# The later layers' pieces in the attention: two parts behind a first half's scores, or four lots behind a second half's

## What is computed

```python
x = inputs.reshape(B, T, NUM_HEADS, HEAD_DIM).transpose(0, 2, 1, 3)
q = x * rotation_params[None, :, None, :]
k = x * entangle_params[None, :, None, :]
attn_weights = jax.nn.softmax(jnp.einsum('bhid,bhjd->bhij', q, k) * scale, axis=-1)
out = jnp.einsum('bhij,bhjd->bhid', attn_weights, x)
...
x = x + _layernorm(_L0_attn_ref(_layernorm(x), ...))   # 4 batches x 16 heads
x = x + _layernorm(_L0_ffn_ref(_layernorm(x), ...))    # token mix, W_r, W_k, relu squared, W_v
x = x + _layernorm(_L1_attn_ref(_layernorm(x), ...))   # linear attention q, k, v, then a 1024-wide MLP
x = x + _layernorm(_L1_ffn_ref(_layernorm(x), ...))    # gate, up, down
```

## Time and profile before

| | us |
|---|---|
| median of 3 runs | 3210.76 (3210.0 to 3214.39) |
| span of the profiled execution | 3210.7 |
| attention, to the last exponential | about 2008 |
| busy: PE, ACT, DVE | 2925.7, 2332.2, 1481.2 |

### The profile page before, as it was taken

One profiled execution on the slowest core, in us unless ns is written; L12 is line 12 of the kernel. 1 busy time (PEld: TensorE's weight loads), 2 busy tenths in 40 slices (PEclk: granted clock), 3 DMA queues, 4 the chain that ended last, 5 costly groups with the idle time before them and its releaser, 6 DMA issues. The chain is left out here.

```text
span 3210.7 us, 48004 instructions
## 1 busy us (share of the span) xinstructions
PE 2925.7 (91%) x18048; PEld 1172.8 (37%) x18048; DVE 1481.2 (46%) x3536; ACT 2332.2 (73%) x2586; POOL 214.9 (7%) x193
## 2 busy tenths in 40 slices
PE   1998998999999999999999999489999999999986
PEld 0221221222222222222222222266666666666654
DVE  6221220322441333232421311668888888866574
ACT  2999999999999999999999999223343334333332
POOL 0000000000000000000000000111111111111110
PEclk9999999999999999999999999699999999999998
DMA  3411111311211221111210110221122111111010
GB/s 115 141 41 36 59 39 36 101 37 35 89 37 35 83 68 42 57 42 43 69 55 28 45 42 21 81 66 53 53 78 66 59 59 59 46 56 50 26 47 21
DMA packets 125601, 177.69 MB, mean 55 GB/s; under 512 B 42248, under 2 KB 100616, under 8 KB 125128
## 3 DMA queue, kind: packets, MB, share of 16 engines
q1 hardware_dynamic: 122392, 172.53, 16.7%
q10 hardware_dynamic: 2992, 2.23, 0.2%
HBM read 107.62 MB, written 67.11 MB: 54 GB/s over the span
## 5 line engine op out<-in xcount | busy, mean ns | idle before, releaser
L717 ACT ACTIVATE probs<-ps 128x1024 f32<-128x1024 f32 x2048 | 1894.4, 1173 | 87.0 <-PE ps L456 83.6
L585 PE MATMUL ps<-probs,vals 128*32 128x512 f32 x8192 | 1094.2, 607 | 0.0
L456 PE MATMUL ps<-qT,kT 64*128 64x512 f16 x4096 | 730.3, 387 | 109.8 <-DMA kT<-split_dram 28.1
L456 PEld LDWEIGHTS ps<-qT,kT 64*128 64x128 f16 x4096 | 173.5, 93 | 1152.0 <-ACT probs L717 1025.3
L872 DVE COPY sums<-ps 128x512 f32<-128x512 f32 x64 | 44.3, 692 | 502.3 <-PE ps L585 502.3
L585 PEld LDWEIGHTS ps<-probs,vals 128*32 128x32 f32 x8192 | 162.0, 108 | 294.2 <-issue 232.8
L1310 PE MATMUL layers_ps<-yT,weight_mem 128*128 128x512 f32 x512 | 227.6, 595 | 11.2 <-ACT hT L1551 10.0
L1316 PE MATMUL layers_ps<-weight_mem,hT 128*128 128x256 f32 x1024 | 231.5, 380 | 0.0
L1578 ACT ACTIVATE gate<-layers_ps 128x512 f32<-128x512 f32 x96 | 57.3, 597 | 224.9 <-PE layers_ps L1464 224.8
L1316 PEld LDWEIGHTS layers_ps<-weight_mem,hT 128*128 128x128 f32 x1024 | 193.0, 190 | 29.8
L1464 PE MATMUL layers_ps<-n4T,weight_mem 128*128 128x512 f16 x768 | 176.7, 384 | 7.3 <-DVE n4T L1801 7.3
(11 more groups left out here) (224 smaller groups left out, 2607.6 us busy)
## 6 DMA issues: line engine op xcount, KB each, us to landing
split_dram<-parts SPq DMA_DIRECT2D x28, 768.0 KB, 3.7
qT<-split_dram SPq DMA_DIRECT2D x126, 128.0 KB
kT<-split_dram SPq DMA_DIRECT2D x126, 128.0 KB
heads_dram<-result SPq DMA_DIRECT2D x64, 128.0 KB, 7.4
q_in<-q_dram SPq DMA_DIRECT2D x16, 512.0 KB, 3.3
n_in<-n_dram SPq DMA_DIRECT2D x16, 512.0 KB, 3.4
x_in<-x_dram SPq DMA_DIRECT2D x16, 512.0 KB, 5.2
out_dram<-y_out SPq DMA_DIRECT2D x16, 512.0 KB, 4.3
```

Of the source, the lines that this page charges most:

```text
L456: last = nc.tensor.matmul(SCORES[slot][:, n * BANK:(n + 1) * BANK], kT[buf][rows, j * P:(j + 1) * P], qT[buf][rows, q0:q0 + BANK], start=T ...
L585: mm = nc.tensor.matmul(ACC[32 * c:32 * c + 32, :], vals[buf][:, j, :], probs[:, j % PROBS, c * BANK:(c + 1) * BANK], start=(j == 0), stop ...
L717: nc.scalar.activation(probs[:, j % PROBS, half * T // 2:(half + 1) * T // 2], SCORES[slot_of(at)], ACT.Exp, scale=OPERAND_SCALE ** -2).th ...
```

## The change

`PART_GAP = 3` gives way to `LOTS_AT = (0, 1, 3, 4)`. A piece now goes to PE in four lots of half the size of a part, and each lot stands behind the second half's scores of a block: the starting block, the next, and the ones three and four later. A lot of a matmul piece is one matmul of 256 columns (two records), one of `kv` is two, one of a transposing piece is one transpose. The second and fourth lots complete what the first and third began in the bank.

```diff
-PART_GAP = 3
+LOTS_AT = (0, 1, 3, 4)
...
-                half = TURN.rearrange("p (b n) -> p b n", b=2)[:, part, :]
+                first, second = part // 2, part % 2
+                half = TURN.rearrange("p (b n) -> p b n", b=2)[:, first, :]
...
-                        for k in range(K4):
-                            last = nc.tensor.transpose(TURN[:, k * P:(k + 1) * P], src[:, k, h * P:(h + 1) * P], ident[:, :])
-                        last.then_inc(fr_full, 1)
-                    return
+                    last = nc.tensor.transpose(TURN[:, part * P:(part + 1) * P], src[:, part, h * P:(h + 1) * P], ident[:, :])
...
-                    for k in range(KC):
-                        last = tok_out(half, fr_uT, 2 * int(stage[-1]) + part, w, k)
+                    last = tok_out(half, fr_uT, 2 * int(stage[-1]) + first, w, second)
...
-                if part == 1:
+                if part == len(LOTS_AT) - 1:
                     last.then_inc(fr_full, 1)
...
-                    for part in range(2):
-                        step = front_step(head, j - PART_GAP * part)
-                        if half == 0 and step is not None:
-                            front(step, part, head, rounds_at(head, j - PART_GAP * part))
+                    for part, after in enumerate(LOTS_AT):
+                        step = front_step(head, j - after)
+                        if half == 1 and step is not None:
+                            front(step, part, head, rounds_at(head, j - after))
```

More of the change, by code:

```diff
@@ L521, in front @@
                         pe.wait_ge(ready, c + 1)
-                        for k in range(K4):
-                            last = nc.tensor.transpose(TURN[:, k * P:(k + 1) * P], src[:, k, h * P:(h + 1) * P], ident[:, :])
-                        last.then_inc(fr_full, 1)
-                    return
-                if stage in ("mix_r0", "mix_r1"):
+                    last = nc.tensor.transpose(TURN[:, part * P:(part + 1) * P], src[:, part, h * P:(h + 1) * P], ident[:, :])
+                elif stage in ("mix_r0", "mix_r1"):
                     if part == 0:
@@ L529, in front @@
                         pe.wait_ge(layer_sem("mixed"), c + 1)
-                    for k in range(KC):
-                        last = tok_out(half, fr_xr, 2 * int(stage[-1]) + part, W["wr"], k)
+                    last = tok_out(half, fr_xr, 2 * int(stage[-1]) + first, W["wr"], second)
                 elif stage in ("mix_k0", "mix_k1"):
                     i = int(stage[-1])
-                    last = nc.tensor.matmul(TURN, W["wk"][:, part, i * P:(i + 1) * P], fr_xk[:, part, :], start=(part == 0), stop=(part == KC - 1))
+                    last = nc.tensor.matmul(half, W["wk"][:, second, i * P:(i + 1) * P], fr_xk[:, second, first * N // 2:(first + 1) * N // 2],
+                                            start=(second == 0), stop=(second == KC - 1))
                 elif stage in ("val0", "val1"):
@@ L537, in front @@
                         pe.wait_ge(layer_sem("k_act_done"), c + 1)
-                    for k in range(KC):
-                        last = tok_out(half, fr_kact, 2 * int(stage[-1]) + part, W["wv"], k)
+                    last = tok_out(half, fr_kact, 2 * int(stage[-1]) + first, W["wv"], second)
                 elif stage in ("k0", "k1", "v0", "v1"):
@@ L543, in front @@
                     w = W["akv"][:, :, 0:C] if stage[0] == "k" else W["akv"][:, :, C:2 * C]
-                    for k in range(KC):
-                        last = tok_out(half, fr_uT, 2 * int(stage[-1]) + part, w, k)
+                    last = tok_out(half, fr_uT, 2 * int(stage[-1]) + first, w, second)
                 elif stage in ("q0", "q1"):
                     i = int(stage[-1])
-                    last = nc.tensor.matmul(TURN, W["aq"][:, part, i * P:(i + 1) * P], fr_uT[:, part, :], start=(part == 0), stop=(part == KC - 1))
+                    last = nc.tensor.matmul(half, W["aq"][:, second, i * P:(i + 1) * P], fr_uT[:, second, first * N // 2:(first + 1) * N // 2],
+                                            start=(second == 0), stop=(second == KC - 1))
                 elif stage == "kv":
@@ L552, in front @@
                         pe.wait_ge(layer_sem("k_feat_done"), c + 1)
-                    for k in range(K4):
-                        last = nc.tensor.matmul(TURN[:, part * KVW:(part + 1) * KVW], fr_k[:, k, part * P:(part + 1) * P], fr_v[:, k, part, :],
+                    for k in range(second * K4 // 2, (second + 1) * K4 // 2):
+                        last = nc.tensor.matmul(TURN[:, first * KVW:(first + 1) * KVW], fr_k[:, k, first * P:(first + 1) * P], fr_v[:, k, first, :],
                                                 start=(k == 0), stop=(k == K4 - 1))
-                if part == 1:
+                if part == len(LOTS_AT) - 1:
                     last.then_inc(fr_full, 1)
```

## The result

| | before | after |
|---|---|---|
| median of 4 runs, us | 3212.57 (3210.0 to 3216.24) | 3224.98 (3223.09 to 3229.99) |
| span of the profiled execution | 3210.7 | 3224.0 |
| heads 18 to 63 without 31 and 47 | 1330.46 | 1348.11 |
| heads 31 and 47 | 71.46 | 70.12 |
| behind the attention | 1202.7 | 1201.0 |

The changed kernel takes 1.0041 of the time before (95% interval 1.0027 to 1.0055), 12.4 us more. 3231 was forecast, with 3215 to 3240 around it. A head's time is the distance between the ends of the last exponentials of two heads; heads 31 and 47, which hold the branches to other code, stand apart.

The account below looks back on a forecast made before the run. ACT's own pace, 29.33 us a head, bounds the attention; about 32 us are waits for scores. Block 2 3.6, rounds 2.6, block 10 2.7 and the head's end 10.8 make 19.7, about +20 on 3210.7: 3231, range 3215 to 3240.

Parts of the forecast that it names:

- block 2: 33 pieces starting in block 2: lots lose 0.58 us a piece for 0.39 to 0.53, together +3.6.
- block 10 with the head's end: 19 pieces starting in block 10: +2.7 us for their own losses, +10.8 where the last lot meets the head's end.
- the 19.7: Sum of the forecast's terms in us: 3.6 + 2.6 + 2.7 + 10.8, taken as +20 on 3210.7.
- The lot's cost: Each matmul lot on PE delays the value product by 0.64 us, a transposing lot about 0.27; weight loads not hidden.
- the cheap lots: Rival: fixed cost of entering and leaving is hidden, a lot costs +0.43 us; 12 us faster, 3199; chance 0.08.
- the reserve: A first half's scores may start 0.78 us late before ACT loses time; PE makes up 0.30 a block.
- Rounds: In 9 heads with a round behind a block-2 piece, block 8's transposes lose 0.29 us each: +2.6.
- The late read: Head's end, 9 block-10 pieces with two-instruction reads: DVE copies the sums some 0.5 us late; 5 to 6 in all.
- A read too late: Rival: block-2 pieces finish later and DVE's chain moves, costing 1 to 2 us in 6 heads; 3240; chance 0.08.
- the operands' copies next: Under the late-read rival: head 35's room of 1.2 us holds narrowly, with these DVE copies next in line.
- ACT's own activations: Heads 37, 59, 61, 63: activations right behind their input's last lot may wait up to 0.5 us each, left to the range.

Follow-up runs that it names:

- gap4: Kernel before, with the second part of block-2 matmul pieces in heads without a round four blocks behind the first instead of three: 3208.14 us, 0.9989.
- block2_lots: Changed kernel's lots only for pieces that start in block 2; those starting in block 10 go in two parts as before: 3220.25 us, 1.0022 of before.
- lots_first_half: Changed kernel with its four lots behind the first half's scores instead of the second's: 3232.57 us, 1.0063 of before.
- block10_lots: Changed kernel's lots only for pieces that start in block 10; those starting in block 2 go in two parts as before: 3223.0 us, 1.0036 of before.
- lots_0123: Changed kernel with lots behind blocks 0, 1, 2 and 3 instead of 0, 1, 3 and 4: 3232.44 us, 1.0071 of before.
- gap4_gap2: gap4, but head 57 keeps a gap of three blocks and block-10 pieces have their second part two blocks behind the first: 3205.19 us, 0.9982 of before.
- the second pair: Both kernels run and profiled again unchanged: before 3211.99 us, changed 3228.31 us (1.0046).

## Why the prediction was right, point by point

The sign, the mechanism and the range held. Three terms of the sum were off: block 2, block 10 with the head's end, and waits that it leaves out. They nearly cancel, so it is in part luck that the 44 heads' 17.65 stands so near the 19.7. The lot's cost and the losses at single exponentials are no luck.

**The lot's cost: right in size, its reading of the weight loads not.** A lot costs 0.63 for 0.64, in `mix_k` and `q` as in `k`, and a transposing lot 0.26 for 0.27; the cheap lots' 0.43 did not come. What halving costs shows beside it: 1.06 to 1.07 for a part, 2 x 0.63 for two lots. But the prediction has the loads of a part as not hidden, and inside a part they are. A `mix_k` part before has two records of 512 columns and two loads, where a `k` part has four of 256 and four loads. PE's timeline of the kernel before, head 43:

```profile
1376.18 1.13 PE L534 MATMUL ps<-fr_xk,weight_mem 128*128 128x512 f32 x2
1377.24 0.39 PE L456 MATMUL ps<-qT,kT 64*128 64x512 f16 x2
```

From its start to the next scores is 1.06, beside 1.07 in the earlier trace rows: two loads more cost nothing. The rule of the Trainium skill that weight loads overlap with matmuls only where row groups differ (TensorE: Matmul & The Clock Gate, Part 3, "The mechanism") does not agree with this. That the queue pulls loads ahead, in the page's table at the top, does. What the 0.10 on entering and the 0.10 on leaving are made of, and whether the first load has a share in them, no run shows.

ACT's timeline, head 41, shows the places where delays pass the reserve, as forecast: none stands out at 12 and 18, and one does at exponential 20 (1325.57), followed by the one behind the round's transposes (1327.69).

```profile
1297.54 27.81 ACT L714 ACTIVATE probs<-ps 128x1024 f32<-128x1024 f32 x30 [0.18 <-PE ps L456]
1325.57 1.94 ACT L714 ACTIVATE probs<-ps 128x1024 f32<-128x1024 f32 x2 [0.23 <-PE ps L456]
1327.69 13.15 ACT L714 ACTIVATE probs<-ps 128x1024 f32<-128x1024 f32 x14 [0.18 <-PE ps L456]
```

The losses of such a piece are 0.18 at exponential 14, 0.03 at 18 and 0.33 at 20; 0.20, 0.04 and 0.34 were forecast.

**Block 2: +3.6 forecast, +1.4 measured** in the 44 heads. Exponentials 14, 18 and 20 lose 20.3, less 3.8 for the activations at 20 and 0.9 for their waits: 15.6 rather than 17.9, beside 14.2 at 12 and 18 (forecast 14.3). I counted 33 pieces; two of them lie in heads 31 and 47, and an activation of ACT's own stands at exponential 20 in four others and takes their 0.33. The price for a piece was right, the count was not.

**Rounds: +2.6 forecast, +2.6 measured** (exponential 22, nine heads, 0.29 each).

**Block 10 and the head's end: +2.7 and +10.8 forecast; +10.5 measured together.** The exponentials from 28 over the head's end to 6 lose 35.1 for 21.9, which is 13.2; 0.9 of it are the activations' waits, 1.4 the late operands and 0.4 the late read, both below. (The prediction's 15.7 for 5.0 is 10.7.) The late read is there, and its mechanism as told. DVE's and PE's timelines of the changed kernel at the end of head 43, behind a `mix_k` piece of two reads:

```profile
1401.48 0.69 DVE L913 TENSOR_SCALAR fr_xr<-ps 128x512 f32<-128x512 f32 x1 [7.68 <-PE ps L531]
1402.21 0.69 DVE L914 TENSOR_TENSOR fr_xr<-fr_xr 128x512 f32<-128x512 f32 x1
1403.14 0.69 DVE L869 COPY sums<-ps 128x512 f32<-128x512 f32 x1 [0.24 <-DVE fr_xr L914]
```

```profile
1400.75 0.70 PE L531 MATMUL ps<-fr_xk,weight_mem 128*128 128x256 f32 x2
1401.38 1.06 PE L582 MATMUL ps<-probs,vals 128*32 128x512 f32 x8
...
1403.89 0.66 PE L633 MATMUL ps<-ident,sums 128*128 128x128 f32 x4 [0.91 <-DVE sums L869]
```

The copy starts 2.39 behind the last lot (2.3 forecast; of the 0.3 for semaphores, for which the prediction shows no row, the copy's wait of 0.24 is the most), and the transposes 2.51 behind the last value product (2.4). But only five heads lose over 1 us at exponential 6: 30, 44, 48, 52 and 63 lose 1.04 to 1.27, where 0.63 is a late head's end with one read. That makes 2.4 for DVE's part, where I had 5 to 6 on nine pieces. Behind the other four of the nine pieces, in heads 22, 32, 59 and 61, an own activation at exponential 4 comes first, and its 0.94 leaves 0.10 to 0.56. **The step that failed here is the multiplication: a price worked out in one head was taken for all, without a look at where ACT's own activations give PE time.**

**A read too late: held at 0.08, and true in part.** It was to cost 1 to 2 us in six heads; it cost 0.4 in head 35 and 1.4 in head 58, and a further four times 0.43. In head 35 (DVE's and PE's timelines, the round's reads and the block-10 piece, before):

```profile
1148.03 0.74 DVE L788 TENSOR_SCALAR qk<-ps,k_factor 128x512 f32<-128x512 f32 x1
```

```profile
1148.87 0.68 PE L551 MATMUL ps<-fr_v,fr_k 128*128 128x130 f32 x4 [0.38 <-DVE qk L788]
```

The lot starts 0.10 behind the end of the read, 0.76 instead of 0.32 behind the scores. The room of 1.2 was used up and 0.4 more: exponentials 28 and 30 lose 0.62 here and 0.21 at the `kv` piece of head 57. At the end of head 57 (PE's and DVE's timelines):

```profile
1832.40 1.06 PE L582 MATMUL ps<-probs,vals 128*32 128x512 f32 x8
1835.10 0.61 PE L456 MATMUL ps<-qT,kT 64*128 64x512 f16 x4 [1.63 <-DVEq L864]
```

```profile
1829.85 4.95 DVE L1048 TENSOR_REDUCE widest_weight<-weight_mem 128x1 f32<-128x4608 f32 x1
1834.72 0.28 DVE L832 COPY vals<-xs 128x256 f32<-128x256 f32 x1
```

gap4 and block2_lots show this wait too, and lots_first_half one of 1.41. In these three and in the changed kernel the block-2 piece of head 57 is complete in block 6. block10_lots, lots_0123 and gap4_gap2, where it is complete in block 5, are without it. The prediction names "the operands' copies next", but I looked for them in no head.

**ACT's own activations.** Heads 37, 59, 61 and 63 lose 1.37 instead of 0.94, together 1.7; "up to 0.5 each" was left to the range. The one in head 37 waits 0.32 for DVE, on ACT's timeline:

```profile
1204.85 1.06 ACT L671 ACTIVATE fr_q<-fr_q 128x1024 f32<-128x1024 f32 x1 [0.32 <-DVEq L940]
```

**The sum.** 1.4 + 2.6 + 10.5 = 14.5 for the 19.7 forecast, and 3.5 for waits that it leaves out: 18.0. The heads' times give 17.65; the table counts only what is over 0.01.

**Outside the 44 heads: 0 forecast.** In the profiled pair they give 4.3 back, in the second pair 2.4 (15.3 of span for 17.67). Behind the attention, where the kernels do the same work, 1.7 to 2.0 us of it lie. The windows over the 130 us behind the last exponential, of the changed kernel and of before (clock in the third column from the right):

```profile
2023.00:2153.00 130.00, 71.07 (x275) 48.08 (x268) 85.05 (x249) 35.30 (x32) 16.94 (x16) 0.79 0.24 70
```

```profile
2008.00:2138.00 130.00, 71.15 (x265) 47.03 (x258) 85.20 (x249) 33.93 (x30) 16.94 (x16) 0.75 0.25 70
```

By 2153 the changed kernel's PE has done ten records more, at a granted clock of 0.79 rather than 0.75. The other profiles agree with this. Where the clock over these 130 us is 0.75 (six profiles), the time behind the attention is 1202.7 to 1203.5; at 0.78 (lots_0123, gap4) it is 1201.7 and 1201.8; at 0.79 (the changed kernel, twice) 1201.0 and 1200.9. That the clock is the cause is still argued, not shown, since no run changed it alone.

Heads 31 and 47 gain 1.3 to 2.0. PE's timelines show where, head 31 before and then changed:

```profile
1017.01 1.47 PE L456 MATMUL ps<-qT,kT 64*128 64x512 f16 x6 [4.09 <-issue]
```

```profile
1018.14 0.82 PE L456 MATMUL ps<-qT,kT 64*128 64x512 f16 x6 [3.30 <-issue]
```

At the branch PE stands idle for 4.09 in head 31 and 4.31 in head 47 before, and for 3.30 and 3.58 in the changed kernel: 1.5 less together, 2.2 less in the second pair. What sets the length of this idle time no run shows. With the start's scatter, these two stretches are why the medians lie at 3225 to 3228 and not nearer 3231.

## What to carry to other kernels

Where an engine is late only by a reserve that refills block by block, cutting work into smaller lots adds each lot's entry and exit and takes away the blocks in which it refills: fewer, larger interruptions, further apart and away from the point where the next queue waits, were faster here. A per-piece price must be multiplied by the pieces that meet it, so list the heads where another engine's own work already gives the time. Whatever delays a piece also delays everything queued behind its reader; look for the longest instruction in that queue (here 4.95 us) and who waits behind it.

## What the runs showed of the hardware

**A wait of 1.4 to 2.0 us was followed by a lower clock once in five times.** At the end of head 57 PE stood 2.02 us in block2_lots and then worked for 1.6. From 1829.9 to 1833.3 the granted clock was 0.50, which is 1.2 GHz, and then 1.00 again, which is 2.4. Exponentials 1 and 2 of head 58 lost 0.47 and 1.55, where the changed kernel lost nothing and 0.34. After waits of 1.41 in lots_first_half, 1.63 and 1.64 in the changed kernel's two profiles and 1.70 in gap4 at the same spot it stayed at 1.00. The idle times of 2.9 to 4.5 us at the branches in heads 7, 15, 31 and 47 have a stretch at 0.50 beside them in every profile.

**The time behind the attention goes with its clock.** In its profiled execution block10_lots took 1212.1 us behind the attention for the 1202.7 before, with the same instructions. The two kernels' windows over 400 us near the end, block10_lots and then before:

```profile
2819.20:3219.20 400.00, 365.04 (x1706) 240.78 (x1705) 255.55 (x637) 133.44 (x184) 46.10 (x36) 0.95 0.12 39
```

```profile
2808.00:3208.00 400.00, 354.20 (x1702) 234.51 (x1700) 257.40 (x640) 131.54 (x181) 46.06 (x36) 0.97 0.12 39
```

PE is busy 10.8 longer with four records more, at a lower granted clock. The kernel's six runs lie in two groups, 3219.8 to 3223.3 and 3232.2 to 3233.1, and the profiled one is of the second, so its median of 3223.0 tells less than its heads do. The kernel before has such runs too: 3 of its 17 beside gap4_gap2 took 3220.0 to 3222.2, at a mean granted clock of 0.977 and 0.978 where the others have 0.981 and 0.982. What sets this off was not tried.

**The attention repeats to hundredths.** 44 heads, 1330 us, agreed within 0.03 us between two executions of a kernel, on a program whose median moves by some us between sets of runs. A question on one stage is best put to that stage.
